# A first phase of signs and convolution: packing on VectorE, all subtractions of means on GpSimd, and the second part of x loaded behind the means

## The reference, cut to what matters

```python
def _ln_c(v, eps=1e-06):
    m = jnp.mean(v, axis=1, keepdims=True)
    s = jnp.var(v, axis=1, keepdims=True)
    return (v - m) / jnp.sqrt(s + eps)

def _L0_conv_ref(x, w, b, gamma, beta):
    xa = sign_a(x)                     # sign
    wq = quant_weight_W2(w)            # sign of the centred weights, times alpha
    y = jax.lax.conv_general_dilated(xa, wq, window_strides=(1, 1), padding=[(1, 1), (1, 1)], ...)
    y = y + b[None, :, None, None]
    mean = jnp.mean(y, axis=(0, 2, 3), keepdims=True)
    var = jnp.var(y, axis=(0, 2, 3), keepdims=True)
    y = (y - mean) * jax.lax.rsqrt(var + EPS)
    y = y * gamma[None, :, None, None] + beta[None, :, None, None]
    return jax.nn.relu(y)

x = x + _L0_conv_ref(_ln_c(x), ...)
```

## Time and profile before

| | |
|---|---|
| median of 3 runs | 2020.09 us (2017.94 to 2023.11) |
| the profiled execution: its time, its span | 2015.51 us, 2013.7 us |
| mean granted TensorE clock | 0.977 of full speed |
| busy over the span | PE 92%, PEld 49%, DVE 78%, ACT 60%, POOL 57% |
| the first phase, without its start and end, 57.30 to 344.30 us | PE busy 253.59 of 287.00 us |
| DMA in that stretch | 16 engines 82% busy, 297 GB/s |

### The profile page before, as it was taken

How to read it: one execution, slowest core, us unless ns; L and a number is a source line. 1 busy time by engine, 2 the same in 40 slices (tenths; PEclk the granted TensorE clock), 3 DMA queues, 4 the chain that set the end, 5 groups by cost and what they waited for, 6 DMA issues and landing times.

```text
span 2013.7 us, 32702 instructions
## 1 busy us (share of the span) xinstructions
PE 1852.1 (92%) x8507; PEld 992.6 (49%) x8507; DVE 1568.3 (78%) x4488; ACT 1214.9 (60%) x2030; POOL 1143.0 (57%) x907
## 2 busy tenths in 40 slices
PE   7789989759999999999999999999999999999996
PEld 4557666634444444444444444444444444444443
DVE  3487677867888788888888888888888888888875
ACT  5466666446666566666666666666666666666653
POOL 3465666364655556556565556665666555555543
PEclk8899999969999999999999999999999999999998
DMA  5677888511333333333333333333333333333213
GB/s 221 246 280 289 295 331 304 199 40 65 129 119 127 110 125 118 118 118 118 122 123 122 125 119 117 119 134 116 119 117 119 125 122 117 120 127 124 99 71 133
DMA packets 82074, 294.08 MB, mean 146 GB/s; under 512 B 23920, under 2 KB 28864, under 8 KB 81984
## 3 DMA queue, kind: packets, MB, share of 16 engines
q1 hardware_dynamic: 68880, 242.40, 33.0%
q10 hardware_dynamic: 13104, 50.72, 6.7%
HBM read 213.80 MB, written 78.07 MB: 145 GB/s over the span
## 4 chain that ended last, share of the span: by engine, by line
PE 51%; DMA 10%; DVE 6%; SPq 6%; issue 3%; POOL 1%; ACT 1%; ACTq 0%; DVEq 0%; POOLq 0%
PE ps L1168 25%; PE ps L1157 6%; PE ps L1158 5%; PE ps L1159 5%; PE ps L1113 5%; SPq L504 4%; DMA wse<-w_row 4%; DMA w_row<-wrow 3%; PE ps L1146 2%; DMA y16a<-y_int 2%; DMA y16b<-y_int 2%; SPq L510 1%; DVE base L910 1%; POOL rm L592 1%; ACT hs L670 1%
## 5 line engine op out<-in xcount | busy, mean ns | idle before, releaser
L1168 PE MATMUL ps<-hs,w_c 128*128 128x448 f32 x1792 | 765.9, 555 | 0.4 <-ACT yo L680 0.4
L670 ACT ACTIVATE hs<-ps,b1c,undo 128x448 f32<-128x448 f32 x896 | 609.8, 719 | 128.6 <-PE ps L1159 121.7
L578 POOL TENSOR_TENSOR tl<-tr,th 128x448 f16<-128x448 f32 x224 | 243.7, 1089 | 306.1 <-PE ps L1159 187.7
L1168 PEld LDWEIGHTS ps<-hs,w_c 128*128 128x128 f32 x1792 | 313.9, 191 | 209.3 <-issue 177.6
L573 POOL TENSOR_TENSOR xb<-xb,zr 128x448 f32<-128x448 f32 x224 | 261.4, 1169 | 265.6 <-ACT zr L697 264.9
L1157 PE MATMUL ps<-th,w_h 128*128 128x448 f16 x896 | 318.4, 355 | 17.0 <-ACT hs L670 17.0
L585 POOL TENSOR_TENSOR yo<-yo,base 128x448 f32<-128x448 f32 x221 | 277.1, 1260 | 75.6 <-DVE yo L987 75.6
L1159 PE MATMUL ps<-th,w_l 128*128 128x448 f16 x896 | 316.1, 353 | 0.0
L1158 PE MATMUL ps<-tl,w_h 128*128 128x448 f16 x896 | 316.1, 353 | 0.0
L680 ACT ACTIVATE yo<-ps,cols 128x448 f32<-128x448 f32 x224 | 141.7, 633 | 240.0 <-PE ps L1168 239.8
L1074 PE MATMUL ps<-packs,cwT 128*128 128x448 f32 x1008 | 245.9, 397 | 1.7 <-DVE y16a L759 1.7
(11 more groups left out here) (146 smaller groups left out, 2376.5 us busy)
## 6 DMA issues: line engine op xcount, KB each, us to landing
xb<-x SPq DMA_DIRECT2D x48, 896.0 KB, 4.6
xb<-x SPq DMA_DIRECT2D x48, 672.0 KB, 4.4
result<-yo SPq DMA_DIRECT2D x32, 896.0 KB, 3.5
gate_all<-gate_row ACTq DMA_DIRECT2D x31, 896.0 KB, 4.4
result<-yo SPq DMA_DIRECT2D x32, 672.0 KB, 3.0
gate_all<-gate_row ACTq DMA_DIRECT2D x31, 672.0 KB, 5.5
base<-x SPq DMA_DIRECT2D x16, 896.0 KB, 10.1
hs<-mean_row SPq DMA_DIRECT2D x14, 896.0 KB, 5.1
```

Source lines behind the costliest of these rows:

```text
L578: nc.gpsimd.tensor_tensor(cut(tl, c), tr[(b + c) % 2][:, :], cut(th, c), ALU.subtract).then_inc(tl_ready, 1)
L670: nc.scalar.activation(hs[(b + slot) % 2][:, j, :], ps[:, H_BANK + j, 0:T], ACT.Gelu_apprx_tanh, bias=b1c[:, j:j + 1], scale=undo[:, 1:2]) ...
L1168: last = M(bank, w2_c[:, j, :], hs[(b + c) % 2][:, j, :], start=first, stop=final)
```

## The change

Four things change in the first phase. DVE packs two signs in one instruction (second times 3072 plus first), in the place of ACT's multiplication and POOL's addition; ACT's multiplication is gone. POOL makes all eight subtractions of a pair, DVE none. In SP's list the load of part 1 of pair p+2 moves from the head of the turn to behind the mean broadcasts of that pair. In the diff `packed`, `signed` and `levelled` are counters that the engines wait on.

```diff
@@ save_mean (SP)
                 if n // 2 >= MEAN_FROM + 2:
-                    sp.wait_ge(levelled, (n // 2 - MEAN_FROM - 1) * 2 * (HALF - 1))
-                    sp.wait_ge(levelled_last, (n // 2 - MEAN_FROM - 1) * 2)
+                    sp.wait_ge(levelled, (n // 2 - MEAN_FROM - 1) * 2 * HALF)
@@ phase1 (SP)
             def phase1(p):
+                if p:
+                    store_y(p - 1, 1)
+                if MEAN_FROM <= p + 2 < NP:
+                    for n in (2 * p + 4, 2 * p + 5):
+                        save_mean(n)
                 if p + 2 <= NP:
                     sp.wait_ge(signed, (p + 1) * 2 * NCH)
                     if p + 2 < NP:
...
-                if p:
-                    store_y(p - 1, 1)
-                if MEAN_FROM <= p + 2 < NP:
-                    for n in (2 * p + 4, 2 * p + 5):
-                        save_mean(n)
                 store_y(p, 0)
@@ POOL
-            def pack(q, c):
-                if c == 0:
-                    pool.wait_ge(border_clear, 2)
-                    if q > 1:
-                        pool.wait_ge(conv_done, (q - 1) * NCH)
-                pool.wait_ge(signed, signs_upto(q, c, 0))
-                pool.wait_ge(scaled, q * NCH + c + 1)
-                first, second = (sgn[k][(q * NCH + c) % 2][:, :].rearrange("p (r w) -> p r w", w=SIDE) for k in range(2))
-                nc.gpsimd.tensor_tensor(pk[q % 2][:, 1 + c * ROWS:1 + (c + 1) * ROWS, 1:1 + SIDE], second, first,
-                                        ALU.add).then_inc(packed, 1)
-
             for q in range(NP):
-                for c in range(NCH):
-                    if q >= MEAN_FROM and c < HALF - 1:
+                if q >= MEAN_FROM:
+                    for c in range(HALF):
                         for k in (1, 0):
                             level(2 * q + k, c)
-                    if c:
-                        pack(q, c - 1)
-                pack(q, NCH - 1)
@@ sign (ACT)
-                act.wait_ge(signed, signs_upto(q, c, 1))
-                nc.scalar.activation(sgn[1][chunk % 2][:, :], sgn[1][chunk % 2][:, :], ACT.Copy,
-                                     scale=PACK).then_inc(scaled, 1)
@@ DVE
-            def level_last(n):
-                q = n // 2
-                dve.wait_ge(mean_in[n % 4], 16 * ((q - MEAN_FROM) // 2 + 1))
-                x_c = cut(xs[n % 4], HALF - 1)
-                V.tensor_tensor(x_c, x_c, mean_cut(n, HALF - 1), ALU.subtract).then_inc(levelled_last, 1)
+            def pack(q, c):
+                if c == 0:
+                    dve.wait_ge(border_clear, 2)
+                    if q > 1:
+                        dve.wait_ge(conv_done, (q - 1) * NCH)
+                dve.wait_ge(signed, signs_upto(q, c, 0))
+                first, second = (sgn[k][(q * NCH + c) % 2][:, :].rearrange("p (r w) -> p r w", w=SIDE) for k in range(2))
+                V.scalar_tensor_tensor(pk[q % 2][:, 1 + c * ROWS:1 + (c + 1) * ROWS, 1:1 + SIDE], second,
+                                       PACK, first, ALU.mult, ALU.add).then_inc(packed, 1)
@@ phase1 (DVE)
-                    if c == HALF - 1 and MEAN_FROM <= p + 1 < NP:
-                        for k in (1, 0):
-                            level_last(2 * p + 2 + k)
                     if c:
                         batch_stats(p, c - 1)
                     elif 0 < p < NP - 1:
                         batch_stats(p - 1, NCH - 1)
+                    for q, d in signs_at(p, c):
+                        pack(q, d)
                     decode(p, c)
...
+            for c in range(2):
+                pack(0, c)
             phase1(0)
```

More of the change, by code:

```diff
@@ L238, in block_kernel @@
         packed = sem("packed")
-        scaled = sem("scaled")
         high_taken = sem("high_taken")
@@ L246, in block_kernel @@
         levelled = sem("levelled")
-        levelled_last = sem("levelled_last")
         centred = sem("centred")
@@ L615, in sign @@
                     if by_mean(q, c):
[L616 to L619, removed]
+                        act.wait_ge(levelled, (q - MEAN_FROM) * 2 * HALF + 2 * c + 2 - k)
                         z = cut(xs[n % 4], c)
```

## The result

| | before | after |
|---|---|---|
| median | 2019.0 us (2015.6 to 2023.1, 4 runs) | 2051.9 us (2046.9 to 2053.2, 4 runs) |
| the profiled execution, its span | 2015.5, 2013.7 us | 2053.1, 2050.9 us |

The ratio is 1.0157, with a 95% interval of 1.0131 to 1.0184. The change makes the kernel 32.9 us slower; 32.7 were forecast.

What follows compares the result with a forecast made beforehand. The first phase was taken as bound by a ring through SP's queue, not PE. Ten turns +26.4, earlier turns +7.9 and the phase's end -1.6 gave +32.7 us, so 2053 us against the 2020.1 median; range 2022 to 2067.

Steps and rivals of the forecast that it cites:

- The ring through SP's queue: First phase: mean broadcasts, next x load, PE's means, copy and save set the 21.8 us turn, not PE's 19.7.
- Part 1 ahead of part 0, +3.2 us in the link: SP's queue, second broadcast to PE's means: part 1's transfers delay part 0, 12.6 + 3.2 = 15.8 us; the deciding term.
- both lulls: Two slack spells of the DMA engines around the first broadcast, taken to lie before the second, so hiding nothing of part 1.
- The link from the means to the next broadcast: PE's means through DVE's copy and store to next first broadcast: stays 4.4 us, packs taking what the emptier queue gives.
- Ten turns, +26.4: First phase, ten turns from 131.10 to 348.67: 24.4 us each, 244 - 217.6 = +26.4 us.
- The turns up to the preparation, +7.9: Turns before 131.10: means at 99.50 come 5.6 us later, DVE's packs less subtractions add 2.3; together +7.9 us.
- The end of the phase, -1.6: PE's 1.64 us wait at 374.44 for signs behind a subtraction DVE no longer makes goes away: -1.6 us.
- PE's wait: PE waiting for x ahead of the means: some 4.5 us a turn, over 3.5 us in nearly every turn.
- The pack, taken at 0.75 us: DVE's packing instruction: 0.75 us each, between bounds 614 and 1281 ns; 5.3 us a pair.
- The first (part 0 not held up by part 1): Rival in SP's queue: moved loads fit in the lulls, turn 20.2 us, 21 us less, 1999 us; chance 0.10.
- The second (DVE the bound): Rival on DVE: packs at 1.28 us, copy of means and ring 1.1 us later, 2068 us; chance 0.15.
- The third (it cancels): Rival: half of 3.2 us hides, emptier queue gives 1 us, turn 22.3 us, 2020 to 2026 us; chance 0.10.

Runs made afterwards that it cites:

- the list alone: Kernel before with only the two blocks of SP's list exchanged, part 1 of x loaded behind the mean broadcasts: 2047.2 us, ratio 1.0163.
- the list put right: Changed kernel with the load of part 1 moved to the turn's end, behind the stores and the next pair's part 0: 2018.2 us, ratio 1.0003.
- half the bytes: Changed kernel with one of the two loads of part 1 ahead of the next pair's part 0, the other behind it: 2035.9 us, ratio 1.0094.
- a shorter first link: Kernel before with both images' means saved together, waited for once and broadcast one behind the other: 1999.0 us, ratio 0.9914.
- the compute parts alone: Changed kernel with SP's list in its old order, leaving packs on DVE, no ACT scaling, subtractions on GpSimd: 2017.8 us, ratio 1.0002.

## Why the prediction was right, point by point

- **What bounds the phase.** The ring through SP's queue, shown in four ways: the list alone makes the loss, the list put right takes it back, half the bytes give 1.4 of the 2.7 us, and a shorter first link makes the kernel before faster.
- **Part 1 ahead of part 0, +3.2 us in the link.** Measured 16.3 - 13.1, which is 3.3 before rounding. The forecast started from the one turn shown, 12.6, where the mean of ten is 13.1. It also took both lulls to lie in front of the second broadcast; the second one reaches 0.6 us behind its issue (the two zeros of the earlier trace rows end at 246.0, the issue is at 245.42), and nothing of part 1 hid in that.
- **The link from the means to the next broadcast, forecast unchanged at 4.4.** Measured 4.6 before and 4.0 after: the emptier queue gave more than the packs took. With the list alone the link is 3.8, and with the compute parts alone 4.8; so the compute parts cost this link 0.2 us a turn under either list, where the forecast let the packs take about 1. Of the link, save to broadcast went from 2.3 us to 1.7; DVE's copy starts 1.7 us behind the start of the means before and after, where 2.15 was forecast for after. These two misses, 0.5 and 0.4, cancelled: the turn was forecast at 24.4 and came to (382.57 - 138.05) / 10 = 24.5.
- **Ten turns, +26.4.** Measured 244.5 - 217.6 = +26.9.
- **The turns up to the preparation, +7.9.** Measured 138.05 - 131.10 = +7.0. The means at 99.50 came at 103.74, +4.2 and not +5.6, and the rest took 2.7 us more, not 2.3. The compute parts show a cost here: the turn with the preparation is 28.8 us with them alone and 25.5 before, though they reach it 2.3 us sooner.
- **The end of the phase, -1.6.** This failed. From the last first broadcast to the end of the phase it is 402.0 - 348.67 = 53.3 us before and 436.7 - 382.57 = 54.1 after, +0.8. PE's wait for the sign went as forecast, but its wait for a decode, behind DVE's aggregation of the statistics (5.8 us), grew from 1.74 us to 3.17. I had looked at one wait and not at the next one in line. DVE now has a pack in every round. Its aggregation starts 2.4 us into PE's last three convolutions ahead of the wait, where it started 1.5 us into them, and one more pack stands between it and the decode:

```profile
421.30 3.93 PE L1056 MATMUL ps<-packs,cwT 128*128 128x448 f32 x12 [3.17 <-DVE y16a L740]
```

  The three parts come to 26.9 + 7.0 + 0.8 = 34.7 us in the profiled executions, where 32.7 were forecast. That the medians differ by 32.9, within 0.2 of the forecast, is in part chance: the profiled execution before lies 3.5 us under its median and the one after 1.2 above.
- **PE's wait, forecast at some 4.5 us a turn (24.4 - 19.7 is 4.7).** Measured 3.6. Behind most of the waits PE runs at a lower clock for a while: at 256.19, behind 3.23 us of idling, the means take 3.21 us and the next two convolutions 5.20, where behind 1.89 us they take 1.71 and 4.05. The granted clock in the stretches from these two starts on (busy columns as in the earlier trace rows):

```profile
256.19:264.54 8.35, 8.35 (x35) 5.30 (x36) 5.59 (x11) 1.50 (x4) 0.00 (x0) 0.65 0.41 149
280.41:286.10 5.69, 5.69 (x35) 4.06 (x36) 5.47 (x11) 1.47 (x3) 0.00 (x0) 1.00 0.30 87
```

  It is 0.65 in the one, a mix of the levels of 1.2 and 2.4 GHz, and 1.00 in the other, with the same 35 matmuls. Most of those 2.7 us lie in time that PE would otherwise have waited. But the means are themselves a link of the ring, and DVE's copy waits for them: the link from the means to the next first broadcast is 4.11 us behind 256.19 and 3.78 behind 280.41. Of the ten turns the six whose means took 3.0 us or more have 4.1 there and the other four 3.8, some 2 us together. That the clock may add to the ring was in the range and not in the sum; it added those 2 of the 33.
- **The pack, taken at 0.75 us.** Measured 0.72, as a mean over the phase:

```profile
L731 DVE SCALAR_TENSOR_TENSOR packs<-sgn 128x448 fp32r<-128x448 bf16 x112 | 80.8, 722 | 16.0 <-ACT sgn L606 16.0
```

  The mean hides two kinds. While GpSimd stands still a pack takes 0.61 us, the lower bound; beside a subtraction it takes up to 1.58 over the phase, and 1.48 in this turn, where GpSimd subtracts from 269.01 on:

```profile
256.56 0.61 DVE L731 SCALAR_TENSOR_TENSOR packs<-sgn 128x448 fp32r<-128x448 bf16 x1
257.09 0.62 DVE L740 SCALAR_TENSOR_TENSOR y16a<-y16b,ps 128x448 f16<-128x448 int16 x1
257.98 0.62 DVE L722 COPY ur<-ps 128x448 f32<-128x448 f32 x1 [0.28 <-PE ps L1044]
...
270.28 1.48 DVE L731 SCALAR_TENSOR_TENSOR packs<-sgn 128x448 fp32r<-128x448 bf16 x1
...
278.26 0.95 DVE L731 SCALAR_TENSOR_TENSOR packs<-sgn 128x448 fp32r<-128x448 bf16 x1
...
269.01 9.71 POOL L541 TENSOR_TENSOR xb<-xb,hs 128x448 f32<-128x448 f32 x8 [14.72 <-DMA hs<-mean_row]
```

  The rule of the Trainium skill (page "SBUF — State Buffer", section "Who interferes with whom"), that a DVE instruction with two SBUF inputs contends with a GpSimd instruction that reads SBUF, agrees with these rows. But it did not decide: the two packs ahead of the copy of the means fell where GpSimd was idle, and the copy at 257.98 waited only for PE.
- **The rivals.** The first (part 0 not held up by part 1) is refuted by the landings, part 1 coming down 6.5 us before part 0 in the turn shown, and by the link, which is 15.9 us or more in each of the ten turns. The second (DVE the bound) is refuted by the compute parts alone, 2017.8 us against 2017.2. The third (it cancels) by the link of 16.3 us.

## What to carry to other kernels

Where an engine waits for a load, look for a ring: that load, what the engine makes from it, what is saved and read back, and what is issued behind that on the same queue. In a queue that works in the order of issue, a transfer costs its own time to everything behind it (here 1.5 to 1.8 us for each load of 672 KB); so the one that nobody waits for goes behind the one that the ring needs, where it also fills the time in which the ring has nothing to move. Count a shortened link against its neighbours: a wait taken out of an issuing engine can come back as time in the queue.

## What the runs showed of the hardware that was not expected

- About half of what is saved by issuing two large transfers 0.4 us apart, and not with a wait between them, comes back: of 3.7 us less between the two issues, 1.7 to 1.9 us reappear in the next link.
- How long PE waited does not tell by itself whether its clock falls. In the change it fell behind a wait of 3.23 us and not behind one of 1.89. In the kernel before the means took 3.21 us behind a wait of 3.66 and 2.74 behind one of 2.10, but 1.71 behind 2.55 and 2.93. With part 1 behind part 0 they took 1.71, at a granted clock of 1.00, behind a wait of 3.21. What decides was not found. The fall at 256.19 cost PE 2.7 us and the ring 0.3.
